# First of four chunks of a recurrent two-layer block: the counts of its third and fourth piece are turned by DMA in place of TensorE

## The chip, the cores and the metric

One core of one Trainium2 chip runs the whole kernel. The metric is the device time of one execution in microseconds. Before the change it is 657.09 us, the median of three executions (655.59 to 657.26).

## What is computed

The input is 4 sequences of 512 rows of 512 numbers. Two layers follow each other, each as `x = x + s * silu(f)` on the layer-normed rows. Only the first layer matters here:

```python
xn = _layernorm(x)
s = _L0_attn_ref(xn, mask, weight, bias)      # one product with a block-masked 512x512 weight
# _L0_ffn_ref, on the rows xf:
inter = xf @ c1_w.T @ c2_w.T                  # rank 16, 1792 columns
blk = inter.reshape(B * T, n_blocks, SPARSITY)             # 56 segments of 32 columns
idx = jnp.argmax(blk, axis=-1) + jnp.arange(0, INTER, SPARSITY)
h = relu(einsum('bkm,bm->bk', w1[idx], xf))
out = einsum('bk,bkm->bm', h, w2t[idx])
x = x + s * silu(out)
```

So in each segment of 32 hidden columns only the first column that holds the largest value of `inter` is used. The second layer is an attention with a routed LoRA; the change doesn't touch it.

## The kernel before

**Chunks and tiles.** A chunk is one sequence of 512 rows. The first layer runs over 4 chunks (the first is written out on its own, the second and third are a loop, the fourth stands alone), then the second layer over the same 4. Within a chunk the rows are four tiles `tt` of 128, and the 1792 hidden columns are 14 blocks `it` of 128. Products are made in three matmuls each, from a rounded high part and a low remainder (`three`, line 418). For each `it` TensorE makes the up product (12 matmuls of 128x512 into `up`), and two steps later the down product (12 matmuls into the four banks `acc`).

**The selection.** The dense 512x1792 hidden activation is made, and then masked. The columns of `inter` come in four pieces `p` of 512, 512, 512 and 256 columns, that is of 4, 4, 4 and 2 blocks `it`. For each piece and each row tile, TensorE makes one matmul (`select`, line 1197) and VectorE makes three instructions: the largest of each segment (`seg_top`, line 918), the comparison (`eq`, line 920), and a scan (line 932) that counts matches from the start of each segment, so that the first match has the count 1. The counts stand with rows on the partitions, the hidden activation `h` has hidden columns on them, so the counts have to be turned. Then VectorE multiplies `h` by (count == 1) (line 953, the *mask* below), ScalarE rounds `h` to `h_hi` (line 755), and VectorE makes `h_lo = h - h_hi` (line 962). ScalarE's relu of the next block (line 734) writes the same `h`, and so waits for `h_lo`. TensorE's down product of the block waits for `h_lo` too.

**Two ways to turn.** In the chunks after the first, SyncE issues one DMA transpose for each piece and row tile (`turn`, line 480), from `counts` to `first` in SBUF. In the first chunk TensorE turns: `first_transpose(it)` (line 1216) makes four transposes of 128x128 in bf16 into a PSUM bank, `first_bank`, for each `it`, behind the select matmul and ahead of the down product of `it - 1`. The counts of an even piece lie in `counts` there and those of an odd one in `first[:, 1]`.

**What else runs there.** In the first chunk GpSimd makes the low parts of the weights: `w1_rest` (line 585) and `w2_rest` (line 590), one tensor_tensor of 128x512 each, behind ScalarE's rounding (lines 702 and 707), which stands behind the relu of a block: that of block `it` is followed by the roundings for `w1` block `it + 4` and `w2` block `it + 2`. Behind the last of these GpSimd halves a bias (line 601), adds it to four tiles (`head`, line 608), and then makes the reciprocal root of the next chunk's variance (`rows_rstd`, lines 380 and 382). For that, VectorE has made the statistics of the next chunk's rows at blocks 6 to 10. VectorE's `rows_norm` (line 388) stands between its work for block 12 and that for block 13 and waits for `rows_rstd`. TensorE's turn of the normed rows (line 348) waits for that, VectorE's `rows_lo` (line 362) follows, and TensorE's `rank_product` (line 1175) opens the next chunk when the last `rows_lo` is through.

**What sets the order.** Each engine runs its own program in the order written out in the kernel, and waits on semaphores. `sel_count` counts scans, `first_tr` counts groups of TensorE's transposes, `h_masked` counts masks, `h_split` counts `h_lo`, and `ld_first[tt]` gets 16 from each DMA transpose of a row tile.

## Time and profile before

| | us |
|---|---|
| time, median of 3 executions | 657.09 |
| lowest and highest of the 3 | 655.59, 657.26 |
| the profiled execution, its own time | 658.42 |
| its span in the trace | 656.6 |
| TensorE busy | 636.8 (97%) |
| VectorE busy | 446.4 (68%) |
| GpSimd busy | 239.5 (36%) |

The profile is that of one execution, and its times are counted from its span's start. The mean granted clock of TensorE is 0.991 of full speed, so it is at its upper level. The page's busy shares are averages over the whole kernel. The first chunk's blocks run from about 38 to 118 us, and what the change touches lies between 77 and 118 us. The timeline of each engine in that stretch is the view to read, with the idle time before each group and what ended it, and the chain of work that ended last.

### The profile page before, as it was taken

To read this page: it belongs to the slowest core of one execution; us is meant where nothing else is said; L and a number is where in the kernel's file an instruction comes from. 1 tells how busy PE (TensorE), PEld (TensorE's weight loads), DVE (VectorE), ACT (ScalarE), POOL (GpSimd) and SP (SyncE) were. 2 spreads that over 40 slices of the span, in tenths; PEclk is the share of its full clock that TensorE was granted. 3 is DMA by queue.
4 is the path that set the end of the run, shared out by engine and by line. 5 is a ranking of instruction groups with operands and counts; after the bars stand their busy time and mean duration, and the time that the engine had idled before them with its cause. 6 is when DMAs were issued, how large, how long until landed. Compare 5 with 4: busy or idle time off the path is not lost.

```text
span 656.6 us, 8460 instructions
## 1 busy us (share of the span) xinstructions
PE 636.8 (97%) x2942; PEld 513.6 (78%) x2942; DVE 446.4 (68%) x716; ACT 213.6 (33%) x379; POOL 239.5 (36%) x185
## 2 busy tenths in 40 slices
PE   7999999999999999999998998999999999999997
PEld 3777888878888878888866886778878878887887
DVE  7986766777765876756877676565665757575633
ACT  3543343322223312224222144452145135314610
POOL 2355545640000820000943056391515333351441
PEclk9999999999999999999999998999999999999999
DMA  8940000123200124100236222031140013002000
GB/s 264 405 161 1 1 0 1 33 80 102 75 13 5 48 64 152 24 12 4 72 107 205 59 77 68 17 122 55 48 141 5 16 43 134 0 32 96 2 32 34
DMA packets 42575, 46.16 MB, mean 70 GB/s; under 512 B 25072, under 2 KB 25456, under 8 KB 41904
## 3 DMA queue, kind: packets, MB, share of 16 engines
q1 hardware_dynamic: 42544, 45.76, 21.3%
q8 instruction: 18, 0.29, 0.2%
q14 instruction: 13, 0.11, 0.1%
HBM read 31.85 MB, written 8.39 MB: 61 GB/s over the span
## 4 chain that ended last, share of the span: by engine, by line
PE 80%; DVE 12%; issue 3%; DMA 2%; ACT 1%; POOL 1%; SPq 0%; DVEq 0%; POOLq 0%; ACTq 0%
PE bank L418 72%; DVE counts L932 3%; PE bank L348 2%; DVE seg_top L918 2%; DVE eq L920 2%; PE bank L1197 1%; PE bank L1351 1%; DMA first<-counts 1%; PE bank L1175 1%; DVE h L953 1%; PE bank L1314 1%; DMA b_raw<-in_lora_b 1%; DVE h_lo L962 1%; POOL g_tile L394 1%; PE bank L1216 1%
## 5 line engine op out<-in xcount | busy, mean ns | idle before, releaser
L418 PE MATMUL bank<-w_hi_t,h_hi 128*128 128x512 f32 x224 | 91.9, 410 | 3.3 <-DVE h_lo L962 3.0
L755 ACT ACTIVATE h_hi<-h 128x512 fp32r<-128x512 f32 x56 | 35.4, 632 | 165.9 <-DVE h L953 165.9
L418 PE MATMUL bank<-w_lo_t,h_hi 128*128 128x512 f32 x224 | 89.1, 398 | 0.0
L418 PE MATMUL bank<-w_hi_t,h_lo 128*128 128x512 f32 x224 | 88.8, 397 | 0.0
L418 PE MATMUL bank<-xT_hi,w_hi_t 128*128 128x512 f32 x224 | 87.6, 391 | 0.0
L418 PE MATMUL bank<-xT_lo,w_hi_t 128*128 128x512 f32 x224 | 87.3, 390 | 0.0
L418 PE MATMUL bank<-xT_hi,w_lo_t 128*128 128x512 f32 x224 | 87.2, 389 | 0.0
L394 POOL TENSOR_TENSOR g_tile<-g_tile,s_tile 128x512 f32<-128x512 f32 x31 | 46.3, 1493 | 93.8 <-DVE g_tile L975 48.9
L932 DVE TENSOR_TENSOR_SCAN counts<-restart,eq 128x512 bf16<-128x512 bf16 (+1 forms) x56 | 75.3, 1344 | 2.4
L918 DVE TENSOR_REDUCE seg_top<-bank 128x16 f32<-128x512 f32 (+1 forms) x64 | 39.5, 618 | 49.8 <-PE bank L1197 49.8
L669 POOL TENSOR_TENSOR prod_lo<-prod,prod_hi 128x512 fp32r<-128x512 f32 x32 | 40.6, 1292 | 57.8 <-ACT prod_hi L793 57.8
L962 DVE TENSOR_TENSOR h_lo<-h,h_hi 128x512 fp32r<-128x512 f32 x56 | 41.5, 741 | 29.3 <-ACT h_hi L755 27.7
L380 POOL TENSOR_TENSOR rstd<-mean_var,eps 128x4 f32<-128x4 f32 x8 | 1.6, 203 | 157.9 <-DVE mean_var L374 157.9
L418 PEld LDWEIGHTS bank<-w_hi_t,h_hi 128*128 128x128 f32 x224 | 42.8, 191 | 13.6 <-DVE h_lo L962 5.1
L418 PE MATMUL bank<-b_hi,prod_hi 128*128 128x512 f32 (+1 forms) x136 | 52.1, 383 | 0.0
L734 ACT ACTIVATE h<-bank 128x512 f32<-128x512 f32 x56 | 33.5, 598 | 55.9 <-DVE h_lo L962 46.5
L418 PE MATMUL bank<-b_hi,prod_lo 128*128 128x512 f32 (+1 forms) x136 | 51.3, 377 | 0.0
L418 PE MATMUL bank<-b_lo,prod_hi 128*128 128x512 f32 (+1 forms) x136 | 51.3, 377 | 0.0
L418 PEld LDWEIGHTS bank<-w_hi_t,h_lo 128*128 128x128 f32 x224 | 42.9, 192 | 9.8
L418 PEld LDWEIGHTS bank<-xT_hi,w_hi_t 128*128 128x128 f32 x224 | 42.2, 188 | 8.8
L418 PEld LDWEIGHTS bank<-xT_hi,w_lo_t 128*128 128x128 f32 x224 | 42.2, 188 | 8.8
L418 PEld LDWEIGHTS bank<-xT_lo,w_hi_t 128*128 128x128 f32 x224 | 42.2, 188 | 8.7
(191 smaller groups left out, 1301.6 us busy)
## 6 DMA issues: line engine op xcount, KB each, us to landing
w_raw<-in_w SPq DMA_DIRECT2D x28, 256.0 KB, 10.2
x_res<-in_x SPq DMA_DIRECT2D x4, 1024.0 KB, 8.4
mid_state<-g_tile SPq DMA_DIRECT2D x16, 256.0 KB, 2.1
x_tile<-mid_state SPq DMA_DIRECT2D x4, 1024.0 KB, 7.3
x_res<-mid_state SPq DMA_DIRECT2D x4, 1024.0 KB, 5.4
out<-g_tile SPq DMA_DIRECT2D x15, 256.0 KB, 2.0
x_tile<-in_x SPq DMA_DIRECT2D x3, 1024.0 KB, 5.6
b_raw<-in_lora_b SPq DMA_DIRECT2D x2, 1024.0 KB, 5.1
```

The source lines that it names most:

```text
L348: last = nc.tensor.transpose(rows_bank(g, tt)[:, k * P:(k + 1) * P], x_tile[:, tt, k * P:(k + 1) * P], ident[:])
L394: nc.gpsimd.tensor_tensor(g_tile[:, tt, :], g_tile[:, tt, :], s_tile[:, tt, :], ALU.mult).then_inc(s_free, 1)
L418: last = nc.tensor.matmul(dst, a, b, start=(start and n == 0), stop=(stop and n == len(mms) - 1))
L669: nc.gpsimd.tensor_tensor(prod_lo[:, kt, :], prod[:, kt % 3, :], prod_hi[:, kt, :].bitcast(F32), ALU.subtract).then_inc(prod_split, 1)
L734: nc.scalar.activation(h[:], up[it % 2][:], ACT.Relu).then_inc(relu_done, 1)
L755: nc.scalar.activation(h_hi[:, it % 2, :], h[:], ACT.Copy).then_inc(h_hi_done, 1)
L918: nc.vector.reduce_max(seg_top[:, 0:segs], got, AX.X).then_inc(seg_max, 1)
L920: nc.vector.tensor_tensor(eq[:, 0:PW[p]].rearrange("p (s n) -> p s n", n=SEG), got, seg_top[:, 0:segs, None].to_broadcast([P, segs, SEG]), ...
L932: nc.vector.tensor_tensor_scan(kept[:, tt, 0:PW[p]], restart[:, 0:PW[p]], eq[:, 0:PW[p]], 0.0, ALU.mult, ALU.add).then_inc(sel_count, 1)
L953: nc.vector.scalar_tensor_tensor(h[:], which, 1.0, h[:], ALU.is_equal, ALU.mult).then_inc(h_masked, 1)
L962: nc.vector.tensor_tensor(h_lo[:, it % 2, :], h[:], h_hi[:, it % 2, :].bitcast(F32), ALU.subtract).then_inc(h_split, 1)
L1175: last = nc.tensor.matmul(sel[:], c1_stack[:, k, :], x[:, k, :], start=(k == 0 and x is xT_hi), stop=(k == KD - 1 and x is xT_lo))
```

## The change

In the first chunk, the pieces 0 and 1 (`BY_PE = 2`) are turned by TensorE as before. The counts of pieces 2 and 3 are written to `counts` and turned by eight DMA transposes from SyncE into `first[:, 0]` and `first[:, 1]`, as in the chunks behind. TensorE's transposes for the blocks 8 to 13 are gone. VectorE's masks of these blocks read `first` in SBUF, not the PSUM bank, and wait for the DMA's semaphores.

```diff
--- before.py
+++ after.py
@@ -431,6 +431,7 @@
         first_bank = banks[7][:].bitcast(BF16)[:, 0:S]
         first_counts = [counts, first[:, 1]]
         NSEL = PIECES * TT
+        BY_PE = 2
         WARM = (28, 4)
         MB = D // SEG
 
@@ -533,8 +534,13 @@
 
             sp.sem_inc(g_free, 1)
             for tt in range(TT):
-                sp.sem_inc(ld_first[tt], PIECES * 16)
+                sp.sem_inc(ld_first[tt], BY_PE * 16)
             next_rows(0, x_rows[1])
+            for p in range(BY_PE, PIECES):
+                if p % 2:
+                    sp.wait_ge(first_tr, 4 * BY_PE)
+                for tt in range(TT):
+                    turn(0, p, tt)
             rows_out(0, mid_rows[0], True)
             with sp.Fori(1, CH - 1) as c:
                 chunk(c, x_rows[c + 1], False)
@@ -924,11 +930,11 @@
             def select_count(c, p, tt):
                 n = p * TT + tt
                 dve.wait_ge(sel_eq, c * NSEL + n + 1)
-                if not opens(c):
+                if not opens(c) or p > BY_PE:
                     dve.wait_ge(ld_first[tt], (c * PIECES + p) * 16)
                 elif tt == 0 and p >= 2:
                     dve.wait_ge(first_tr, 4 * (p - 1))
-                kept = first_counts[p % 2] if opens(c) else counts
+                kept = first_counts[p] if opens(c) and p < BY_PE else counts
                 nc.vector.tensor_tensor_scan(kept[:, tt, 0:PW[p]], restart[:, 0:PW[p]], eq[:, 0:PW[p]], 0.0,
                                              ALU.mult, ALU.add).then_inc(sel_count, 1)
 
@@ -942,7 +948,7 @@
                     if 0 < it < 4 * (PIECES - 1):
                         select(c, it // 4 + 1, it % 4)
                     dve.wait_ge(relu_done, c * IT + it + 1)
-                    if opens(c):
+                    if opens(c) and it < 4 * BY_PE:
                         dve.wait_ge(first_tr, it + 1)
                         which = first_bank
                     else:
@@ -1245,7 +1251,7 @@
                     else:
                         pe.wait_ge(relu_done, c * IT + IT - 1)
                         transpose_rows(pe, c + 1, 0)
-                    if first:
+                    if first and it <= 4 * BY_PE:
                         first_transpose(it - 1)
                     if it >= 2:
                         pe.wait_ge(h_split, c * IT + it - 1)
```

On TensorE, the change as it stands in the program, first the place of block 8, behind `select` of piece 3, row tile 0. In the names, `xT` and `w_hi_t` are operands of the up product, `c_stack` and `t_stack` those of the selection, `h_hi` and `h_lo` those of the down product. Before:

```order
L418 MATMUL bank<-xT_hi,w_lo_t 128x512
L1197 MATMUL bank<-c_stack,t_stack 128x256
L1216 MATMUL bank<-ident_bf,counts 128x128 x4
L418 MATMUL bank<-w_hi_t,h_hi 128x512
L418 MATMUL bank<-w_lo_t,h_hi 128x512
```

After:

```order
L418 MATMUL bank<-xT_hi,w_lo_t 128x512
L1203 MATMUL bank<-c_stack,t_stack 128x256
L418 MATMUL bank<-w_hi_t,h_hi 128x512
L418 MATMUL bank<-w_lo_t,h_hi 128x512
```

The four transposes between the selection and the down product are gone, here and at five more places; nothing takes their place on TensorE.

On VectorE, the work for blocks 8 and 9, with what each instruction waits for. Before:

```order
L932 SCALAR_TENSOR_TENSOR first<-restart,eq 128x256 [waits first_tr,sel_eq]
L953 SCALAR_TENSOR_TENSOR h<-bank,h 128x512 [waits first_tr,relu_done]
L369 BN_STATS bn<-x_tile 128x6
L962 TENSOR_TENSOR h_lo<-h,h_hi 128x512 [waits h_hi_done]
L918 TENSOR_REDUCE seg_top<-bank 128x8 [waits sel_done]
L920 TENSOR_TENSOR eq<-bank,seg_top 128x256 [waits seg_max]
L932 SCALAR_TENSOR_TENSOR first<-restart,eq 128x256 [waits sel_eq]
L953 SCALAR_TENSOR_TENSOR h<-bank,h 128x512 [waits first_tr,relu_done]
```

After:

```order
L938 SCALAR_TENSOR_TENSOR counts<-restart,eq 128x256 [waits ld_first_0,sel_eq]
L959 SCALAR_TENSOR_TENSOR h<-first,h 128x512 [waits ld_first_2,ld_first_1,ld_first_3,ld_first_0,relu_done]
L369 BN_STATS bn<-x_tile 128x6
L968 TENSOR_TENSOR h_lo<-h,h_hi 128x512 [waits h_hi_done]
L924 TENSOR_REDUCE seg_top<-bank 128x8 [waits sel_done]
L926 TENSOR_TENSOR eq<-bank,seg_top 128x256 [waits seg_max]
L938 SCALAR_TENSOR_TENSOR counts<-restart,eq 128x256 [waits ld_first_1,sel_eq]
L959 SCALAR_TENSOR_TENSOR h<-first,h 128x512 [waits relu_done]
```

The instructions and their order are the same. The mask's first input is `first`, no longer a bank, and the waits on `first_tr` are now waits on the DMAs.

On SyncE, from the last load of the first chunk on. Before:

```order
L498 DMA x_res<-in_x 128x4x512
L480 DMA_TRANSPOSE first<-counts 128x4x128
L486 DMA mid_state<-g_tile 128x512
```

After:

```order
L499 DMA x_res<-in_x 128x4x512
L481 DMA_TRANSPOSE first<-counts 128x4x128 x4
L481 DMA_TRANSPOSE first<-counts 128x2x128 x4
L481 DMA_TRANSPOSE first<-counts 128x4x128
L487 DMA mid_state<-g_tile 128x512
```

The eight new transposes stand where SyncE before had nothing to issue until the next chunk's counts.

## Rows read from the trace of the kernel before

**Rows 1.** Chain that ended last, 70 to 130 us: start, us, what

```profile
84.04 5.52 PE bank L418 x24
```

**Rows 2.** Timeline, TensorE: start, us, engine, line, out<-in [idle before <-releaser]

```profile
83.64 0.40 PE L1216 MATMUL bank<-ident_bf,counts 128*128 128x128 bf16 x4
83.85 0.47 PE L418 MATMUL bank<-w_hi_t,h_hi 128*128 128x512 f32 x1
84.16 0.39 PE L418 MATMUL bank<-w_lo_t,h_hi 128*128 128x512 f32 x1
```

**Rows 3.** Timeline, VectorE: the selection's first instruction, first and second chunk

```profile
89.71 0.42 DVE L918 TENSOR_REDUCE seg_top<-bank 128x8 f32<-128x256 f32 x1 [1.38 <-PE bank L1197]
...
95.58 0.42 DVE L918 TENSOR_REDUCE seg_top<-bank 128x8 f32<-128x256 f32 x1 [2.15 <-PE bank L1197]
...
187.16 0.42 DVE L918 TENSOR_REDUCE seg_top<-bank 128x8 f32<-128x256 f32 x1 [1.90 <-PE bank L1197]
...
192.74 0.43 DVE L918 TENSOR_REDUCE seg_top<-bank 128x8 f32<-128x256 f32 x1 [2.00 <-PE bank L1197]
```

**Rows 4.** Timeline, VectorE: from the second chunk's fourth scan to its first mask

```profile
134.33 2.07 DVE L932 TENSOR_TENSOR_SCAN counts<-restart,eq 128x512 bf16<-128x512 bf16 x1
138.98 0.69 DVE L953 SCALAR_TENSOR_TENSOR h<-first,h 128x512 f32<-128x512 bf16 x1 [2.58 <-DMA first<-counts]
```

**Rows 5.** Page part 2: GB/s of all DMA in 40 equal slices of 16.4 us

```profile
GB/s 264 405 161 1 1 0 1 33 80 102 75 13 5 48 64 152 24 12 4 72 107 205 59 77 68 17 122 55 48 141 5 16 43 134 0 32 96 2 32 34
```

**Rows 6.** Line 480 by itself: issue ns min/median/max; then to landing

```profile
L480 SPq DMA_TRANSPOSE first<-counts x48: 1168/1190/2362, 126.0 to 396.8; - x48
...
DMA to landing us min/median/max: 2.3/2.3/5.9
```

**Rows 7.** Line 953 by itself: forms, duration ns min/median/max, first and last start

```profile
L953 DVE SCALAR_TENSOR_TENSOR h<-first,h x42: 665/666/3921, 139.0 to 407.2; 128x512 f32<-128x512 bf16 x42
L953 DVE SCALAR_TENSOR_TENSOR h<-bank,h x14: 657/665/692, 38.9 to 111.5; 128x512 f32<-128x512 bf16 x14
```

**Rows 8.** Timeline, GpSimd, fourth chunk

```profile
353.01 4.48 POOL L622 TENSOR_TENSOR wqkv_lo<-wqkv_raw,wqkv_hi 128x1536 fp32r<-128x1536 f32 x1 [16.93 <-ACT a_hi L714]
```

**Rows 9.** Timeline, VectorE, fourth chunk

```profile
354.12 3.92 DVE L953 SCALAR_TENSOR_TENSOR h<-first,h 128x512 f32<-128x512 bf16 x1
```

**Rows 10.** Timeline, GpSimd, first chunk, blocks 8 to 12

```profile
84.84 1.69 POOL L585 TENSOR_TENSOR w_lo_t<-w_raw,w_hi_t 128x512 fp32r<-128x512 f32 x1 [4.35 <-ACT w_hi_t L702]
86.49 1.29 POOL L590 TENSOR_TENSOR w_lo_t<-w_raw,w_hi_t 128x512 fp32r<-128x512 f32 x1
89.62 1.30 POOL L585 TENSOR_TENSOR w_lo_t<-w_raw,w_hi_t 128x512 fp32r<-128x512 f32 x1 [1.84 <-ACT w_hi_t L702]
...
94.72 1.28 POOL L590 TENSOR_TENSOR w_lo_t<-w_raw,w_hi_t 128x512 fp32r<-128x512 f32 x1 [2.17 <-ACT w_hi_t L707]
100.52 1.29 POOL L590 TENSOR_TENSOR w_lo_t<-w_raw,w_hi_t 128x512 fp32r<-128x512 f32 x1 [4.52 <-ACT w_hi_t L707]
...
102.49 5.87 POOL L608 TENSOR_TENSOR s_tile<-s_tile,bias_a 128x512 f32<-128x512 f32 x4
...
108.60 1.02 POOL L382 TENSOR_TENSOR rstd<-rstd,neg_half 128x4 f32<-128x4 f32 x1
```

**Rows 11.** Timeline, VectorE, first chunk, blocks 7 to 12

```profile
79.38 2.19 DVE L932 TENSOR_TENSOR_SCAN counts<-restart,eq 128x512 bf16<-128x512 bf16 x1
...
85.36 0.67 DVE L953 SCALAR_TENSOR_TENSOR h<-bank,h 128x512 f32<-128x512 bf16 x1
...
86.73 1.60 DVE L962 TENSOR_TENSOR h_lo<-h,h_hi 128x512 fp32r<-128x512 f32 x1
...
91.38 0.66 DVE L953 SCALAR_TENSOR_TENSOR h<-bank,h 128x512 f32<-128x512 bf16 x1
...
98.54 0.69 DVE L962 TENSOR_TENSOR h_lo<-h,h_hi 128x512 fp32r<-128x512 f32 x1 [0.77 <-ACT h_hi L755]
...
109.66 1.92 DVE L388 TENSOR_SCALAR x_tile<-x_tile,mean_var,rstd 128x512 f32<-128x512 f32 x4
```

## The prediction

> **What bounds the kernel now.** I read the chain of work that ended last first, between 70 and 130 us. There it is almost wholly TensorE's: 24 matmuls for 5.52 us [rows 1], a selection, four transposes [rows 2], and again 24 matmuls. So TensorE's order is the path in the first chunk up to block 12, and an instruction less on it is worth its pitch, as long as nobody else comes to be late. Then the timelines of the other engines in the same stretch, to see who is nearly late. VectorE's selection instruction is idle 1.38 and 2.15 us before blocks 9 and 10 in wait of TensorE [rows 3]: VectorE has room there, but little. The third view is GpSimd's timeline, and it holds the second bound. From 100.52 us GpSimd works without a gap: the last weight remainder, the bias, four tiles of `head` for 5.87 us, the two steps of `rows_rstd`, of which the last begins at 108.60 and takes 1.02, to 109.62 [rows 10]. VectorE's `rows_norm` starts at 109.66 [rows 11], 0.04 us behind. Everything up to the next chunk hangs on it: TensorE's turn of the normed rows, the mask of block 13 behind it on VectorE, `h_lo` of 13, `rows_lo`, `rank_product`. So TensorE and GpSimd arrive there together in the kernel before.
>
> **What TensorE saves.** Six groups of four transposes go. The first of block 8's starts at 83.64 and the second down matmul at 84.16, 0.52 us later [rows 2]. Without them, the down product would start where the transposes did, and one matmul pitch, 5.52 / 24 = 0.23 us [rows 1], would lie between. 0.52 - 0.23 = 0.29 us for each group. The second chunk has the same blocks with no transposes on TensorE, which is a second way to read the price: there the selections of blocks 9 and 10 are 192.74 - 187.16 = 5.58 us apart, in the first chunk 95.58 - 89.71 = 5.87 [rows 3]: again 0.29. Six times 0.29 is **1.75 us**, the most that this part can give. Of the first group some 0.2 comes: it frees the down product of block 7, whose `h_lo` is hardly ready (scan to 79.38 + 2.19 = 81.57, from a mask to its `h_lo` 86.73 - 85.36 = 1.37, `h_lo` 0.69: 83.6 [rows 11]).
>
> **What SyncE adds.** Eight DMA transposes. SyncE has nothing else to issue there, so nobody is queued behind a waiting issue: the stores of the chunk come later. One takes 1.19 us to issue and lands 2.3 us from issue [rows 6], and in the second chunk the mask starts 138.98 - (134.33 + 2.07) = 2.58 us behind the end of the fourth scan [rows 4]. For block 8 the fourth scan of piece 2 ends at 79.38 + 2.19 = 81.57, so the counts are there at 84.15, and the mask doesn't begin before 85.36 [rows 11]: 1.2 us of cover. For block 12, the mask, the rounding and `h_lo` of block 11 and a relu lie between the fourth scan of piece 3 and the mask: 1.37 + 0.69 (1.60 if held up) [rows 11] and some 0.7 for the relu, 2.8 to 3.7 us against 2.58, and behind it `rows_norm` waits for GpSimd anyway. So I cost the turning at nothing. If the cover were gone it would cost the lateness once each time. The new waits on `ld_first` in the scans of piece 3 are for transposes issued 4 blocks earlier; nothing.
>
> **What it does to VectorE and GpSimd.** The mask's input changes from a PSUM bank to SBUF. Line 953 takes 665 ns in the median with either input, but its longest is 692 ns with the bank and 3921 ns with `first` [rows 7]. That longest one started at 354.12 and ended at 358.0; a GpSimd tensor_tensor of 4.48 us ran from 353.01 to 357.5 [rows 8, 9]. The mask had stood still until GpSimd was through, and then took its 0.6 us. `h_lo` (two SBUF inputs, `h` and `h_hi`) shows the same in the first chunk: at 86.73 it takes 1.60 us and not 0.69, beside a GpSimd instruction of 86.49 to 87.78 [rows 10, 11]. And GpSimd's instruction at 84.84 takes 1.69 and not 1.29, behind VectorE's scan [rows 10]: a VectorE instruction of this kind holds GpSimd off for 0.40 to 0.45 us. So the masks of blocks 8 to 13, which in the kernel before pass GpSimd freely, will now stand in its way and it in theirs.
>
> The Trainium skill, on the page "SBUF — State Buffer", section "Who interferes with whom", says the same: a VectorE instruction with two SBUF inputs contends with a GpSimd instruction that reads SBUF, whoever is first has the port for its whole instruction, and one with at most one SBUF input doesn't contend. It speaks against this change. By it the sum is the +1.7 us below; were it wrong, the -0.7 of the first rival.
>
> I work the stretch through block by block, with VectorE holding GpSimd off for 0.45 us and GpSimd holding VectorE for 1.25.
> - Block 8: the mask is ready at 85.36, inside GpSimd's instruction of 84.84 to 86.53. It starts at 86.5, 1.15 later. GpSimd's next instruction (86.49) waits 0.45 for it and ends at 88.25; `h_lo` of block 8 waits for that and ends at 88.8, where it had ended at 88.33: **+0.5**. The relu of block 9 and the weight remainder behind it come 0.5 later, so GpSimd's 89.62 becomes 90.15.
> - Block 9: the scan, ready at 90.4, is now behind that instruction, until 91.4; GpSimd's next goes at 91.9, and the mask (ready at 91.9) waits for it until 93.2, where it had begun at 91.38. `h_lo` comes at 94.5: **+1.8**. Here TensorE, 0.5 us ahead by now, waits about 0.3 for `h_lo` of block 9, and VectorE starts its next selection at 95.1, still 0.4 earlier than 95.58 [rows 3].
> - Block 10: the remainder of `w2` block 12 moves from 94.72 [rows 10] to 96.5. The mask is ready at 96.7, behind it, and starts at 97.8. `h_lo` of block 10 goes from 98.54 [rows 11] to 99.3: **+0.75**. The relu of 11 and GpSimd's 100.52 go with it, to 101.25.
> - Blocks 11 and 12, during `head`: in the kernel before 5.87 us for four instructions of 1.29 each, so 0.7 us of being held off. Now the masks of 11 and 12 and `h_lo` of 12 fall into GpSimd's run too, while the scan of block 11 falls ahead of `head`: two more holds than before, 2 x 0.45 = **+0.9**.
>
> `rows_rstd` then ends at 109.62 + 0.75 + 0.9 = 111.3. From `rows_norm` on, all is as before, relative to it: VectorE's mask 13, `h_lo`, `rows_lo` set the end, and TensorE, which arrives about 1 us earlier than before, waits. The end of the first chunk moves by **+1.7 us**. The rest of the kernel follows from `rank_product` and its chain is unchanged, so the time moves by as much.
>
> **Bounds of this.** Below: no contention of the masks. Then the selections of blocks 9 and 10 come 0.2 and 0.5 us earlier, and with the latter `h_lo` of block 10 and GpSimd's last run. It is still GpSimd that ends last, and the sum is -0.6 to -0.7. Above: one more collision, or one lost at its worst place, costs up to 1.25 us, less what it hides: +2.4. Between -0.7 and +2.4 I take +1.7, since the rows of line 953 with `first` are the very instruction.
>
> **Against the measured times.** The sum starts from the profiled execution's own 658.42 us and gives 660.1. That execution is 1.33 us above the median, and above all three timed ones, so the forecast goes by the median: 657.09 + 1.7 = **658.8 us**. The edges of what a measurement can tell from no change, 0.3%, are 1.97 us off: 655.1 and 659.1.
>
> **The rivals.**
> 1. *Masks don't collide, GpSimd's chain still ends last.* For it: most `first` masks take 665 ns. Against: in the second and third chunk GpSimd has nothing to do at these blocks, which is why. 657.09 - 0.7 = 656.4.
> 2. *TensorE alone counts.* All six groups come through: 655.3. It needs `rows_norm` to start early, and the 0.04 us between GpSimd's end and it speaks against that.
> 3. *The turned counts land late (slower).* The mask of block 8 has 1.2 us of cover, so this decides from a landing 3.5 us behind the issue on. The longest landing of the row is 5.9 us [rows 6]; that would put the mask at 87.6, 1.1 behind where the collision puts it, and the later collisions on top: about +3, 660.1. Against it: the fifth to seventh slices of 16.4 us, from 66 to 115 us, move 1, 0 and 1 GB/s [rows 5], so that the transposes have the queue for themselves.
> 4. *The change doesn't do what it says.* The program's order shows TensorE's six groups gone and nothing else moved; I give it nothing.
>
> **Chances.** Forecast 0.70, rival 1 0.17, rival 2 0.05, rival 3 0.08. The forecast's own spread is +1.0 to +2.4, and the three timed executions (655.59 to 657.26) spread by 1.7 us, so two in five of its cases end above 0.3%: 0.28. Rival 3 gives 0.07. That is 0.35 for slower. Faster by 0.3% needs rival 2 and luck: 0.03. The rest, 0.62, is within. The range has to hold the forecast with its spread, 657.3 to 660.2, and rival 1: 656.0 to 660.2.
>
> **What would show it.** In the profile of after: masks of line 959 (953 before) for blocks 8, 9, 10 of 1.1 us and more beside GpSimd instructions; `h_lo` of block 9 starting 1.8 us later; `rows_norm` starting at about 111.3; TensorE idle for 2 us and more before the turn of the normed rows; selections of blocks 9 and 11 some 0.2 and 0.4 to 0.7 us earlier. Masks of 0.67 us throughout and `rows_norm` near 109.0 would be rival 1. A mask of block 8 with idle time ended by the DMA would be rival 3. The weak point is the race at block 10: if the mask comes 0.2 us ahead of GpSimd's instruction, it goes first, and the total falls to about +1.

## The result, and the profile after

The changed kernel takes 661.91 us in the median of six executions (660.03 to 663.45); the kernel before takes 656.41 in the median of its six beside it (655.57 to 657.96). The ratio is 1.0081, with a 95% interval of 1.0057 to 1.0105: slower by 3.7 to 6.9 us. The forecast was 658.8, up to 660.2. The profiled execution of after took 663.03 us, its span is 661.1, against 658.42 and 656.6 before.

The page of after, its first lines, and the group of line 959 (the mask, 953 before):

```profile
span 661.1 us, 8423 instructions
...
PE 636.8 (96%) x2918; PEld 513.4 (78%) x2918; DVE 450.6 (68%) x716; ACT 213.8 (32%) x379; POOL 241.3 (36%) x185
...
L959 DVE SCALAR_TENSOR_TENSOR h<-first,h 128x512 f32<-128x512 bf16 x48 | 42.7, 890 | 11.8 <-DMA first<-counts 8.3
```

The transposes are gone, and TensorE is busy for the same 636.8 us as before. VectorE is busy 4.2 us longer and GpSimd 1.8. The page can't tell more, so I cut both traces at marks that every kernel of the study has. The marks are starts of instructions of VectorE: its `t_stack` instruction, which stands ahead of a chunk's selections (once in each of the four chunks, and taken as the end of the chunk before), the selection of piece 2's last row tile (ahead of block 8), the first of `rows_norm`, and the clearing of `combT`, with which the second layer begins. The length of each stretch, in us:

| | to the first selection | to block 8 | to `rows_norm` | to the end of chunk 1 | chunk 2 | chunk 3 | chunk 4 | layer 2 |
|---|---|---|---|---|---|---|---|---|
| before | 18.24 | 59.69 | 31.73 | 11.63 | 95.68 | 95.79 | 106.94 | 236.90 |
| after | 18.65 | 59.92 | 33.45 | 12.77 | 96.24 | 95.76 | 107.38 | 236.93 |
| difference | +0.41 | +0.23 | +1.72 | +1.14 | +0.56 | -0.03 | +0.44 | +0.03 |

The sum is +4.5, the difference of the spans. The first two columns are older than the change's first effect; I take their 0.64 us off where rows are compared below. Three places are read here: the stretch up to `rows_norm`, the stretch behind it, and the second chunk. The fourth, the last chunk, has a section of its own below.

VectorE in the stretch of the masks, timeline of after (start, us, engine, line, out<-in, [idle before <-releaser]), to be held against [rows 3, 11]:

```profile
86.01 1.72 DVE L959 SCALAR_TENSOR_TENSOR h<-first,h 128x512 f32<-128x512 bf16 x1
...
92.47 1.71 DVE L959 SCALAR_TENSOR_TENSOR h<-first,h 128x512 f32<-128x512 bf16 x1
...
94.88 0.69 DVE L968 TENSOR_TENSOR h_lo<-h,h_hi 128x512 fp32r<-128x512 f32 x1
95.72 0.42 DVE L924 TENSOR_REDUCE seg_top<-bank 128x8 f32<-128x256 f32 x1
...
97.24 1.72 DVE L959 SCALAR_TENSOR_TENSOR h<-first,h 128x512 f32<-128x512 bf16 x1
...
99.73 0.69 DVE L968 TENSOR_TENSOR h_lo<-h,h_hi 128x512 fp32r<-128x512 f32 x1 [0.77 <-ACT h_hi L761]
...
112.02 1.92 DVE L388 TENSOR_SCALAR x_tile<-x_tile,mean_var,rstd 128x512 f32<-128x512 f32 x4 [2.42 <-POOL rstd L382]
```

GpSimd beside it, timeline of after, to be held against [rows 10]:

```profile
87.14 1.75 POOL L596 TENSOR_TENSOR w_lo_t<-w_raw,w_hi_t 128x512 fp32r<-128x512 f32 x1
...
91.97 1.66 POOL L596 TENSOR_TENSOR w_lo_t<-w_raw,w_hi_t 128x512 fp32r<-128x512 f32 x1
...
101.71 1.29 POOL L596 TENSOR_TENSOR w_lo_t<-w_raw,w_hi_t 128x512 fp32r<-128x512 f32 x1 [3.30 <-ACT w_hi_t L713]
...
104.06 6.67 POOL L614 TENSOR_TENSOR s_tile<-s_tile,bias_a 128x512 f32<-128x512 f32 x4
...
110.96 1.02 POOL L382 TENSOR_TENSOR rstd<-rstd,neg_half 128x4 f32<-128x4 f32 x1
```

Three masks take 1.7 us where they took 0.67, each beside a GpSimd instruction. Two of these grew as well, from 1.29 to 1.75 and from 1.28 to 1.55 us; the one between them, of 1.66, had taken 1.68 before, beside a scan. The masks of blocks 11 and 12 take 1.04 and 0.97, and GpSimd's halving of the bias ahead of `head` 1.00 in place of 0.62. `rows_norm` waits 2.42 us for GpSimd. The chain that ended last (start, us, what) shows what this did to the path. It is TensorE's up to block 9, then goes through a scan and a mask that stood still, and from 101.71 on it is GpSimd's, where before it was TensorE's until VectorE's mask of block 12 at 107.5:

```profile
84.44 5.54 PE bank L418 x24
...
91.06 1.49 DVE counts L938
92.55 1.64 DVE h L959
...
101.71 1.29 POOL w_lo_t L596
...
105.62 5.11 POOL s_tile L614 x3
...
113.80 3.72 PE bank L418 x12
```

The last row is new: twelve matmuls for 3.72 us. The same twelve took 2.83 us in the kernel before. TensorE's timeline and its granted clock say why (windows: from:to, us, busy time of the engines, PEclk, DMA share, GB/s):

```profile
109.27 0.39 PE L418 MATMUL bank<-w_hi_t,h_lo 128*128 128x512 f32 x1
112.72 1.08 PE L348 MATMUL bank<-ident,x_tile 128*128 128x128 f32 x4 [3.06 <-DVE x_tile L388]
...
114.45 0.63 PE L418 MATMUL bank<-w_hi_t,h_lo 128*128 128x512 f32 x1
```

```profile
108.00:112.00 4.00, 1.66 (x8) 1.04 (x6) 1.00 (x1) 1.17 (x2) 3.91 (x4) 1.00 0.00 0
112.00:114.00 2.00, 1.28 (x5) 1.25 (x6) 1.98 (x5) 0.00 (x0) 0.00 (x0) 0.59 0.00 0
114.00:118.00 4.00, 4.00 (x18) 3.25 (x17) 1.83 (x3) 1.12 (x3) 0.00 (x0) 0.78 0.00 0
```

TensorE had been idle for 3.06 us. Behind that the granted clock is 0.59 and 0.78 of full speed, a mixture of the level of 1.2 GHz and that of 2.4, and a matmul takes 0.63 us and not 0.39. In the kernel before, the clock is 1.00 in the same windows.

The third place is the second chunk. VectorE's fourth scan and first mask there, to be held against [rows 4], and SyncE's transpose between them:

```profile
137.82 2.07 DVE L938 TENSOR_TENSOR_SCAN counts<-restart,eq 128x512 bf16<-128x512 bf16 x1
143.04 0.69 DVE L959 SCALAR_TENSOR_TENSOR h<-first,h 128x512 f32<-128x512 bf16 x1 [3.15 <-DMA first<-counts]
```

```profile
140.41 1.21 SPq L481 DMA_TRANSPOSE first<-counts  x1
```

The scan ends at 139.89, and SyncE issues 0.52 us later. In the kernel before, the scan ends at 136.40 and the issue stands at 136.50. The mask waits 3.15 us in place of 2.58.

### The profile page after: what moved, and what is told of

It is laid out like the page before. It is cut to its first block, busy times and chain, and to the rows that moved or that the text cites. A ratio compares the mean times of both kernels' runs of the same rounds, so it can differ in the third digit from the quotient of the medians.

```text
span 661.1 us, 8423 instructions
## 1 busy us (share of the span) xinstructions
PE 636.8 (96%) x2918; PEld 513.4 (78%) x2918; DVE 450.6 (68%) x716; ACT 213.8 (32%) x379; POOL 241.3 (36%) x185
## 4 chain that ended last, share of the span: by engine, by line
PE 77%; DVE 12%; issue 4%; POOL 3%; DMA 3%; ACT 1%; SPq 0%; POOLq 0%; DVEq 0%; ACTq 0%
PE bank L418 70%; DVE counts L938 3%; PE bank L348 2%; DVE seg_top L924 2%; DVE eq L926 2%; PE bank L1203 1%; DMA first<-counts 1%; PE bank L1357 1%; DVE h L959 1%; PE bank L1181 1%; DMA x_tile<-in_x 1%; PE bank L1320 1%; POOL s_tile L614 1%; DMA b_raw<-in_lora_b 1%; DVE h_lo L968 1%
## 5 line engine op out<-in xcount | busy, mean ns | idle before, releaser
L938 DVE TENSOR_TENSOR_SCAN counts<-restart,eq 128x512 bf16<-128x512 bf16 (+1 forms) x60 | 79.3, 1321 | 2.5
L959 DVE SCALAR_TENSOR_TENSOR h<-first,h 128x512 f32<-128x512 bf16 x48 | 42.7, 890 | 11.8 <-DMA first<-counts 8.3
L418 PEld LDWEIGHTS bank<-w_lo_t,h_hi 128*128 128x128 f32 x224 | 43.3, 193 | 7.6
```

The costliest lines, as they stand in the source:

```text
L418: last = nc.tensor.matmul(dst, a, b, start=(start and n == 0), stop=(stop and n == len(mms) - 1))
L938: nc.vector.tensor_tensor_scan(kept[:, tt, 0:PW[p]], restart[:, 0:PW[p]], eq[:, 0:PW[p]], 0.0, ALU.mult, ALU.add).then_inc(sel_count, 1)
L959: nc.vector.scalar_tensor_tensor(h[:], which, 1.0, h[:], ALU.is_equal, ALU.mult).then_inc(h_masked, 1)
```

## The experiments

Theory: GpSimd and VectorE hold each other off at the masks that now read SBUF. That delays GpSimd's last run and `rows_norm`. Rivals: the turning by DMA itself costs the time, or the loss lies elsewhere. The length named "first part" is that from the selection ahead of block 8 to `rows_norm` (31.73 before), "second part" that from there to the end of the chunk (11.63 before).

### Contention alone, and the rest without it

`sbuf_mask` is the kernel before with a constant in SBUF as the first input of the masks of blocks 8 to 13; it has no new DMA, and TensorE's transposes stay. `bank_mask` is the changed kernel, where these masks read the bank. Both leave out the right counts of these blocks, and have the same instructions otherwise.

```diff
--- before.py
+++ sbuf_mask.py
-                        which = first_bank
+                        which = first_bank if it < 8 else restart[:]
--- after.py
+++ bank_mask.py
-                        which = first[:, it // 4 % 2, it % 4, :]
+                        which = first_bank if opens(c) else first[:, it // 4 % 2, it % 4, :]
```

> The kernel before, TensorE's transposes kept and no DMA turns in the first chunk; only the first input of the masks of blocks 8 to 13 of the first chunk is changed, from the PSUM bank to a constant tile in SBUF of the same shape and type (so these blocks are masked with other counts, and the transposes made for them are not read). It has the contention between VectorE and GpSimd and nothing else of the change. Theory (the masks' second SBUF input makes GpSimd's chain late): masks of 1.0 to 1.7 us beside GpSimd instructions, rows_norm starts near 111.3 and not 109.7, 658.1 us (657.5 to 659.5). Rival (the DMA turns, or TensorE's missing work, are what costs): rows_norm near 109.7 and the time of before, 656.4 within 0.7.

> The changed kernel with all its DMA turns and without TensorE's six groups, but the masks of blocks 8 to 13 of the first chunk read the PSUM bank as before (which holds the turned counts of block 7, so these blocks are masked with other counts); they still wait for the DMAs. Theory (contention): all masks 0.67 us, rows_norm near 109.0, the first chunk ends 0.6 to 0.7 us earlier than before, 655.7 us (655.0 to 656.4). Rival (the DMA turns cost): the time stays near 661.9.

| | median (range), n | ratio to before, 95% | first part | second part | chunk 2 |
|---|---|---|---|---|---|
| sbuf_mask | 659.25 (657.4 to 663.1), 10 | 1.0028 (1.0005 to 1.0051) | 33.81 | 13.17 | 95.65 |
| bank_mask | 659.23 (657.87 to 661.63), 10 | 1.0016 (0.9987 to 1.0044) | 31.54 | 11.62 | 96.05 |

Contention alone, without TensorE's lead, moves `rows_norm` by 33.81 - 31.73 = +2.08. The turns by DMA and TensorE's lead, without this contention, move it by -0.19. Together they gave +1.72 in after. So the first part's loss is the masks' reading of SBUF, and it comes without any DMA. Of the 0.6 to 0.7 that the lead alone should have given, 0.19 came. A row of bank_mask shows where some of it stayed: GpSimd's first step of `rows_rstd` now falls beside VectorE's `h_lo` of block 12, and takes 0.65 us, not 0.20:

```profile
107.95 0.65 POOL L380 TENSOR_TENSOR rstd<-mean_var,eps 128x4 f32<-128x4 f32 x1
```

The second part of sbuf_mask is longer by 1.54, and its clock falls there too, behind a wait of TensorE of 2.18 us:

```profile
112.44 1.08 PE L348 MATMUL bank<-ident,x_tile 128*128 128x128 f32 x4 [2.18 <-DVE x_tile L388]
```

And bank_mask keeps the longer second chunk, sbuf_mask doesn't: that +0.4 belongs to the turns or to what came with them, not to the masks. By the time bank_mask was a miss: 655.7 us was expected, 659.23 came, and its interval takes in no difference at all. The expectation had the first chunk alone in it; chunk 2 and the last chunk (106.84, below) stand against the shorter first part.

### The clock in the wait

`fill_gap` is the changed kernel with twelve matmuls that nobody reads, ahead of TensorE's wait for the normed rows. `after_again` is the changed kernel once more.

```diff
--- after.py
+++ fill_gap.py
                     else:
+                        if first:
+                            keep_going(12)
                         pe.wait_ge(relu_done, c * IT + IT - 1)
                         transpose_rows(pe, c + 1, 0)
```

> The changed kernel with 12 more matmuls of 128x512 in bf16 on TensorE, results unused, in the 3.06 us in which it waits for the normed rows. Theory (the granted clock falls to half behind that idle time, 0.59 and 0.78 of full in the two stretches behind it, and costs 1.1 us of the 2.9 that the first chunk lost): the granted clock is 1.00 from 112 to 118 us, the twelve down matmuls take 2.8 us and not 3.7, 660.8 us. Rival (the clock costs nothing, since VectorE's chain sets the end there): 661.9, the first chunk ends where it does in the changed kernel.

> The changed kernel as it is, a second time, beside the kernels of this batch, for a second profile and a time on the same chip. Theory (the first chunk loses 2.9 us, the second 0.5, and the rest of the 5.5 us between the medians is the last chunk's, whose length takes one of two values near 104.2 and 106.9 us in the six profiles so far, in any kernel): first chunk +2.9 and second +0.5 against the profile of before, 3.4 us over before by the time (2.5 to 4.5). Rival (there is a third loss of the change): again 5 us over before.

fill_gap: 659.22 us (656.84 to 661.33, n = 10), where 660.8 was expected, ratio 1.0023 (1.0001 to 1.0045), first part 33.43, second part 11.62, clock 1.00. By itself that reads like a proof. But after_again, with no filler, has a first part of 33.43 and a second part of 11.60; its time is 660.96 (659.82 to 664.78, n = 7), ratio 1.0068 (1.0039 to 1.0097). TensorE's wait there, and the clock behind it:

```profile
112.05 0.63 PE L348 MATMUL bank<-ident,x_tile 128*128 128x128 f32 x4 [2.99 <-DVE x_tile L388]
```

```profile
112.00:114.00 2.00, 1.95 (x11) 1.71 (x12) 1.87 (x4) 0.09 (x1) 0.00 (x0) 1.00 0.00 0
```

The same program waited as long (2.99 and 3.06 us), and once the clock fell and once it stayed. So the +1.14 of the first profile is real but doesn't come in every execution, and the 2.9 us that were expected for the first chunk again were 1.7. The first part repeats to 0.02 us.

### Can the gain be had?

In `rstd_early`, GpSimd makes `rows_rstd` ahead of `head`, so that the norm needn't wait for `head`. In `split_head`, the last two tiles of `head` also wait until VectorE has normed the rows.

```diff
--- after.py
+++ split_head.py
             def body(c, last):
-                rows_rstd(gp, c + 1)
+                if not opens(c):
+                    rows_rstd(gp, c + 1)
...
-            head(0)
-            with gp.Fori(0, CH - 1) as c:
+            rows_rstd(gp, 1)
+            head(0, range(0, 2))
+            gp.wait_ge(xn_ready, 2 * TT)
+            head(0, range(2, TT))
+            body(0, False)
+            head(1)
+            with gp.Fori(1, CH - 1) as c:
```

(rstd_early has one `head(0)` in place of the three lines behind `rows_rstd(gp, 1)`.)

> The changed kernel; on GpSimd the reciprocal root of the next chunk's variance stands ahead of the four tiles of head, not behind them, in the first chunk. Theory (GpSimd's chain is the whole loss, and TensorE's six groups are worth 1.7 us where it is not in the way): rows_norm starts right behind h_lo of block 12, no idle TensorE over 1 us, clock 1.00, the first chunk ends 1.0 to 1.7 us earlier than before: 655.0 us (654.5 to 655.8). Rival (the loss is also in the later chunks or in the turns): over 657.

> The changed kernel; on GpSimd in the first chunk rows_rstd stands ahead of head, and the last two tiles of head wait until VectorE's four rows_norm are through. (With rows_rstd ahead alone, rows_norm took 3.82 us in place of 1.92, beside head's instructions.) Theory (that is the port again, the tensor_scalar of rows_norm stands against GpSimd like the masks): rows_norm takes 1.9 us, the first chunk is 1.0 us shorter than before from the last selection of piece 2 to its end (42.2 to 42.7 against 43.36 us). By the time 0.5 us below before, since the second chunk keeps its 0.5 us loss: within 0.3% of before. Rival (something else slows rows_norm): 3.8 us again, 44.1 us.

rstd_early: 660.05 us (657.99 to 663.99, n = 12), ratio 1.0045 (1.0021 to 1.0068), a miss of 5 us against the 655.0 expected. `rows_norm` began 31.73 - 30.62 = 1.1 us earlier than in before, counted from the mark ahead of block 8, but the part behind took 13.50. VectorE's norm, which in before had GpSimd silent beside it, now has `head` there. Its first three tiles take 3.37 us, where all four took 1.92:

```profile
108.78 3.37 DVE L388 TENSOR_SCALAR x_tile<-x_tile,mean_var,rstd 128x512 f32<-128x512 f32 x3
```

split_head gives it the silence back:

```profile
108.52 1.90 DVE L388 TENSOR_SCALAR x_tile<-x_tile,mean_var,rstd 128x512 f32<-128x512 f32 x4
```

Its two parts are 30.61 + 11.93 = 42.54, where before has 43.36: the first chunk is now shorter than before by 0.8. Both kernels show a little of rival 3: VectorE stands idle 0.93 and 0.89 us before the mask of block 12, and the DMA ended that. Most of it would have been there anyway, for ScalarE's relu ended only at 106.14 and 105.89, and the masks began at 106.38 and 106.08. The mask of block 12 in after starts 0.04 us behind its relu, so the late turn costs 0.20 and 0.15 us. SyncE was busy 1.88 and 1.83 us with issuing it, and it landed 3.06 and 3.01 us behind the start of the issue, where 1.2 and 2.3 stood in [rows 6]. The time of split_head is still 657.91 (656.25 to 660.36, n = 12), ratio 1.0022 (1.0007 to 1.0037), and not the 0.5 us below before that was expected. Its chunk 2 is 96.24, and its chunk 4 105.23.

### The last chunk and its clock

Chunk 4 has the same instructions in all of these kernels, but for the fillers of three of them, which are described below. Its length in the profiles:

| clock 1.00 throughout the chunk | clock fell in it |
|---|---|
| 103.12 before_again, 103.06 sp_instr | 106.94 before |
| 103.18 before_fill_last | 107.38 after, 107.16 after_again |
| 103.31 split_fill, 103.23 after_fill_all | 106.84 bank_mask and rstd_early |

The others lie between (104.16 to 105.85), and in each of them the clock fell at one or both of two places: about 360 us, behind TensorE's wait for the `h_lo` that GpSimd's long instruction holds up [rows 8, 9], and about 406 us, behind its wait for the normed rows. The six profiles in which the turned counts of the first chunk come by DMA, with no filler here, all show the fall at the second place. Of the five others without filler, before, sbuf_mask and turns_alone do, before_again and sp_instr don't. The second place, 405 to 410 us, and TensorE's wait ahead of it, in before:

```profile
406.07 1.09 PE L348 MATMUL bank<-ident,x_tile 128*128 128x128 f32 x4 [2.82 <-DVE x_tile L388]
```

```profile
405.00:410.00 5.00, 3.93 (x12) 3.29 (x13) 4.30 (x8) 2.75 (x5) 2.62 (x2) 0.53 0.00 0
```

and in before_again, the same program:

```profile
405.77 0.63 PE L348 MATMUL bank<-ident,x_tile 128*128 128x128 f32 x4 [2.86 <-DVE x_tile L388]
```

```profile
405.00:410.00 5.00, 3.85 (x21) 3.11 (x21) 4.20 (x8) 3.15 (x6) 2.93 (x2) 1.00 0.00 0
```

2.82 and 2.86 us of waiting, 12 matmuls in the window in one and 21 in the other.

In most kernels with the change this wait is also longer. It is 2.82 to 3.10 us in the five profiles of the kinds without it (before, before_again, sp_instr, sbuf_mask, turns_alone), and 2.90 in fill_gap, 3.33 in after_again, 3.68 in after, 3.97 in rstd_early, 3.99 in split_head and 4.03 in bank_mask. In after:

```profile
410.96 1.08 PE L348 MATMUL bank<-ident,x_tile 128*128 128x128 f32 x4 [3.68 <-DVE x_tile L388]
```

ScalarE shows where it comes from. Its rounding of `b_raw`, a weight of the second layer, stands ahead of its rounding of block 12's `h`, and waits for the last load of `b_raw`. SyncE issues that load behind the chunk's last turn. In before and in after:

```profile
403.08 1.15 ACT L727 ACTIVATE b_hi<-b_raw 128x512 fp32r<-128x512 f32 x2 [2.34 <-DMA b_raw<-in_lora_b]
407.96 1.15 ACT L733 ACTIVATE b_hi<-b_raw 128x512 fp32r<-128x512 f32 x2 [3.20 <-DMA b_raw<-in_lora_b]
```

The 0.86 us between 2.34 and 3.20 is the 0.86 between TensorE's waits of 2.82 and 3.68. Why the last turn and the load behind it come late in five of the eight profiles with the change, and in none of the six without, stays open. To see whether the clock is the matter, `before_fill_last` puts fillers into this chunk's two waits, and `split_fill` does it to split_head. `after_fill_all` is the changed kernel with fillers there and in the first chunk's wait.

```diff
--- before.py
+++ before_fill_last.py
+                        if last and it == 6:
+                            keep_going(8)
                         pe.wait_ge(h_split, c * IT + it - 1)
...
+                        if last:
+                            keep_going(12)
                         pe.wait_ge(relu_done, c * IT + IT - 1)
                         transpose_rows(pe, c + 1, 0)
```

> The kernel before with 8 and 12 more matmuls of 128x512 in bf16 on TensorE in the last chunk of the first layer, results unused, in the two places where it stands idle 2.3 and 2.8 us there. Theory (the clock, as in fill_gap): granted clock 1.00 between 360 and 412 us and not 0.83 and 0.5, the last chunk takes 103 to 104.5 us and not 106.9, the time falls by 2 to 3 us. Rival (the clock hides behind VectorE there): no change.

> The two edits together on the changed kernel: split_head in the first chunk, the fillers in the last. Theory: the gains add, first chunk 42.2 to 42.7 us, last chunk 103 to 104.5 us; 2.5 to 3.5 us below before, and within 0.5 us of before_fill_last, since the DMA turns give 1.0 us in the first chunk and cost 0.5 in the second.

> The changed kernel with the fillers of fill_gap in the first chunk and those of before_fill_last in the last, so that TensorE's clock should not fall in any of them; the order of GpSimd is that of the changed kernel. Against before_fill_last (655.1 us) it shows what the change costs without the clock. Theory: 1.7 us of contention in the first chunk and 0.5 in the second, 657.3 us (656.8 to 657.9), with runs that spread by less than 1.5 us; the other 3.6 us of the changed kernel's 660.9 are the clock's. Rival (the runs' other losses are not the clock's): over 659, and the spread stays.

| | median (range), n | ratio to before, 95% | chunk 1 from block 8 on | chunk 2 | chunk 4 | span |
|---|---|---|---|---|---|---|
| before_fill_last | 655.11 (654.67 to 656.53), 12 | 0.9982 (0.9968 to 0.9996) | 43.34 | 95.65 | 103.18 | 654.7 |
| split_fill | 655.09 (654.43 to 656.50, and one of 2260), 12 | 0.9975 (0.996 to 0.999) | 42.52 | 96.22 | 103.31 | 652.7 |
| after_fill_all | 658.86 (656.88 to 660.89), 12 | 1.0024 (1.0006 to 1.0041) | 45.03 | 96.19 | 103.23 | 656.9 |

The row of the same window in before_fill_last has the clock at 1.00:

```profile
405.00:410.00 5.00, 4.68 (x25) 3.35 (x23) 4.22 (x8) 2.81 (x6) 2.32 (x2) 1.00 0.00 0
```

The executions of before in that round lie from 654.6 to 660.1, those of before_fill_last from 654.67 to 656.53: the fillers take the upper part of the spread away. The gain of 0.18% is smaller than the 2 to 3 us expected, which went by the profile of before, in which the clock had fallen at both places. Probably for the same reason split_fill isn't 2.5 to 3.5 us below before, but 0.25%; it is within 0.5 us of before_fill_last, as expected. after_fill_all against before_fill_last compares the change with no change, with the clock at 1.00 in both profiles: 656.9 - 654.7 = +2.2, of which 45.03 - 43.34 = 1.69 is the first chunk and 96.19 - 95.65 = 0.54 the second. By their ratios to before the two are 1.0024 - 0.9982 = 0.0042 apart, 2.8 us, with some 1.5 us of uncertainty to either side: the same within what can be told. By its time after_fill_all was a miss: 657.3 us was expected and 658.86 came, and its executions still spread over 4 us. Two stretches that the change and the fillers don't touch vary by themselves, chunk 3 (95.7 or 96.6) and the one ahead of the first selection (18.2 to 19.7), and give 2 us of such a spread; the rest I can't place.

The mean granted clock is on record for every execution, not only for the profiled ones, and it says more than the profiles do:

| | executions | mean granted clock: range | mean | span, mean |
|---|---|---|---|---|
| before, beside after_again | 29 | 0.992 to 1.000 | 0.9969 | 654.73 |
| after_again | 7 | 0.987 to 0.995 | 0.9926 | 659.69 |
| after, first round | 6 | 0.990 to 0.995 | 0.9918 | 660.03 |
| before_fill_last | 12 | 0.997 to 1.000 | 0.9995 | 653.42 |
| after_fill_all | 12 | 0.995 to 1.000 | 0.9985 | 656.83 |

All 13 executions of the changed kernel have 0.995 or less; of the 103 of before in the four rounds of the experiments 75 have 0.997 or more. So the change does lower the clock, in more than single profiles. An estimate of the cost: 0.9969 - 0.9926 = 0.0043 of 657 us is 2.8 us, at most, since a low clock costs nothing where TensorE isn't waited for. The spans differ by 4.96, so at least 2.1 are left for the rest. With the fillers, 0.0010 or 0.7 us of the 2.8 between the ratios is still the clock's.

(Two executions of before, of 1284 and 791 us, are left out in the table and in these counts.)

### The half microsecond in the second chunk

All kernels with the real turns have it (chunk 2 from 96.05 to 96.34, idle before the mask 3.02 to 3.15), all without don't (95.64 to 95.68, 2.58; 95.79 and 2.62 in turns_alone). Two ways were tried to get it alone, both on before. `sp_instr` gives SyncE 24 more instructions. `turns_alone` gives it eight DMA transposes of a constant, at the same points, to a place that nobody reads then.

```diff
--- before.py
+++ sp_instr.py
             next_rows(0, x_rows[1])
+            for _ in range(24):
+                sp.sem_inc(turns, 1)
--- before.py
+++ turns_alone.py
-                sp.sem_inc(ld_first[tt], PIECES * 16)
+                sp.sem_inc(ld_first[tt], 2 * 16)
             next_rows(0, x_rows[1])
+            sp.wait_ge(c2_split, 2)
+            for p in range(2, PIECES):
+                for tt in range(TT):
+                    sp.wait_ge(sel_count, p * TT + tt + 1)
+                    sp.wait_ge(ld_first[tt], p * 16)
+                    sp.sem_inc(turns, 1)
+                    sp.dma_start_transpose(first[:, 0, 0:PW[p] // P, rows(tt)],
+                                           restart[:, 0:PW[p]]).then_inc(ld_first[tt], 16)
```

> The kernel before with 24 more semaphore increments on SyncE (three for each of the eight turns), no DMA, ahead of the first chunk's stores. It asks why the fourth turn of the second chunk is issued 0.52 us behind its scan in the changed kernels, and 0.10 before. Theory (it is where the instruction stands in SyncE's program): the mask of the second chunk is idle 3.0 to 3.1 us for the DMA, the second chunk takes 96.2 us. Rival (it is the earlier turns themselves): 2.58 us and 95.7 us as before.

> The kernel before as it is, for a second profile. First chunk 43.36 us from the last selection of piece 2 to its end and second 95.7 us, as in the first profile; the last chunk 104 to 107 us, one of the values that it had in the other profiles.

> The kernel before, with the eight DMA transposes of the change added in the first chunk behind the same scans, but turning a constant tile into a place that nobody reads until it is written again; TensorE's transposes and the masks are as before. So it has the turns and nothing else of the change. Theory (the second chunk's loss and the later last load of the last chunk come from the number of turns that went before): first chunk 43.36 us, the second chunk's first mask idle 3.0 to 3.1 us for the DMA and the chunk 96.2 us; the issue of the last turn in the last chunk 1.9 us or more, TensorE idle 3.7 to 4.0 us there and the last chunk 105 to 107.4 us; 657.5 us by the time. Rival (they come from something else of the change): 95.7 us, and the time of before.

sp_instr: 657.44 (654.89 to 658.09, n = 8), ratio 1.0002 (0.9984 to 1.002), chunk 2 95.64. turns_alone: 657.27 (655.65 to 658.79, n = 12), ratio 1.0014 (1.0001 to 1.0026), chunk 2 95.79, and in the last chunk a wait of 3.10 us and not 3.7 to 4.0. before_again: 655.92, chunk 2 95.65; its last chunk, 103.12, lies below the 104 to 107 expected. The second chunk's first mask in turns_alone:

```profile
140.21 0.69 DVE L961 SCALAR_TENSOR_TENSOR h<-first,h 128x512 f32<-128x512 bf16 x1 [2.62 <-DMA first<-counts]
```

Neither the number of SyncE's instructions nor eight more DMA transposes make the +0.5. In all eight profiles that have it, SyncE issues 0.52 us after the scan's end in place of 0.10. Why it does stays open.

## Why the prediction was right or wrong, point by point

- **TensorE's saving**, 0.29 us for a group, and the clear cover of block 8's DMA: right. The selection of block 10 begins at 95.72 - 0.64 = 95.08 in after, 95.1 was worked out. The mask of block 8 has no idle time ahead of it.
- **Contention at the masks**: right in mechanism and, to `rows_norm`, in size, the size with some luck. `h_lo` of block 9 at 94.88 - 0.64 = 94.24 (94.5 forecast), of block 10 at 99.09 (99.3). `head` grew by 6.67 - 5.87 = 0.80 (0.9). `rows_rstd` ended at 111.98 - 0.64 = 111.34 (111.3). +1.72, where +1.7 stood. But GpSimd's run began at 101.71 - 0.64 = 101.07 and not at 101.25, 0.2 early, and the halving of the bias took 0.38 longer, a hold that the forecast didn't have; the two errors nearly cancel. The Trainium skill, page "SBUF — State Buffer", section "Who interferes with whom", has the rule that an instruction of VectorE with two SBUF inputs contends with GpSimd's reads; this case's masks agree (0.67 against 1.72 us), and sbuf_mask shows it with the input alone changed. The prediction took from the same section of the Trainium skill that an instruction with at most one SBUF input doesn't contend, and left out that the section excepts the 2-port performance modes; the norm of rstd_early, with one tensor input, did contend (1.49 us for 0.54).
- **"From `rows_norm` on, all is as before, relative to it"**: this step failed first. The text had seen that TensorE would be idle there for 2 us and more, and booked that as a mere wait. In the profiled execution it cost 1.14 us more, since the granted clock had fallen when TensorE resumed; in the repeated one nothing. The trace of before already held the row that warned of it: the windows behind the wait of 2.82 us at 406 us with a clock of 0.53. In before_again, the same program, nothing followed such a wait, so the row was a warning and no certainty.
- **"The rest of the kernel follows ... its chain is unchanged"**: failed as well. Chunk 2 is 0.5 us longer in each profile with the change. It was not predicted, and its cause isn't found. Chunk 4's length depends on the clock, which fell there in six of six profiles with the change and no filler, in three of five without it, and TensorE's wait there is longer in five of those six. That the change lowers the clock is shown by the executions (13 of 13 at 0.995 or less). How much of that each of the two waits gives, that of the first chunk and that of the last, isn't shown.
- **The sum.** 1.7 + 0.5 = 2.2 us is the change with the clock at 1.00, by the two profiles with fillers. The medians of the kernels without fillers differ by 5.5 in one round and by 660.96 - 656.49 = 4.5 in another. The remaining 2.3 to 3.3 us I put down to the clock behind TensorE's waits, in the first chunk (1.14 where it fell) and in the last (up to 4). For single profiled executions the rows show it. For the medians the estimate from the executions' mean clocks, 2.8 us at most, has the right size, and the fillers bring the difference down to 2.8. The prediction had the clock's part at nothing.
- **The rivals.** Rival 1 needed masks of 0.67 us: wrong, and even where it was forced (bank_mask) its gain to `rows_norm` was 0.19 and not 0.7. Rival 2 was wrong: GpSimd's end decides. Rival 3 didn't occur in after; in rstd_early and split_head it costs 0.15 to 0.2 us at block 12. The forecast's cover of 2.8 to 3.7 us for that block was right: in split_head the relu ended 105.89 - 102.86 = 3.03 us behind the scan. Too small was the 2.58 us for the turn, which took 106.08 - 102.86 = 3.22 to the mask.
- **The range** ended at 660.2, since the forecast's own upper end was the price of one more collision. It had no term for the clock or for anything behind the first chunk.

## What to carry to other kernels

Freeing the busiest engine of work is worth nothing where another chain ends at the same moment, and moving an operand from PSUM to SBUF can lengthen just that chain through an engine that the change never names. When a sum says that the matmul engine will wait longer, read what the granted clock did behind waits of that length elsewhere in the same trace, and put that cost in the range. A few matmuls that nobody reads, placed in such waits, were worth more here (-0.2%, a narrower spread) than the change itself, which needed them and two moved steps to come to the same time.

## What the runs showed of the hardware

- The clock's fall behind a wait of TensorE isn't fixed by the wait's length. It fell behind 2.18, 2.82 and 3.06 us, and stayed at 1.00 behind 2.86 and 2.99. Both pairs, 2.82 and 2.86 in the kernel before and 3.06 and 2.99 in the changed one, are of one place in one program. At a third place, near 360 us, a wait of 2.33 us is followed by a fall in before (0.66 from 360 to 365 us) and by none in before_again (1.00). Each fall made 4 to 12 matmuls of 128x512 take some 0.63 us in place of 0.39.
- A VectorE `tensor_scalar` of 128x512 in float32 from SBUF to SBUF took 0.54 us alone (split_head, four in 1.90) and 1.49 beside GpSimd's `tensor_tensor` (rstd_early, the first two of its four; the other two, as GpSimd's run ended, 0.54). It has one tensor input only. The Trainium skill, page "SBUF — State Buffer", section "Who interferes with whom", counts `tensor_scalar` among those that can take the shared port pair, and the rows agree.
- A mask of 0.67 us made GpSimd's instruction 0.46 us longer (1.75 for 1.29), and was itself 1.05 longer (1.72), so that in this collision VectorE lost more than GpSimd. Whether it costs the kernel anything is decided by what waits for either.
